# V projected straight into its row form for two head pairs at a time, in a float32 differential-attention and expert kernel

## The reference, cut to what matters

```python
Q = jnp.einsum('bse,hec->bhsc', X, Wq) + bq[None, :, None, :]
K = jnp.einsum('bse,hec->bhsc', X, Wk) + bk[None, :, None, :]
V = jnp.einsum('bse,hed->bhsd', X, Wv) + bv[None, :, None, :]
Q1, Q2 = (Q[..., :d], Q[..., d:])          # d = 64
K1, K2 = (K[..., :d], K[..., d:])
A1 = jnp.einsum('bhqd,bhkd->bhqk', Q1, K1) * s
A2 = jnp.einsum('bhqd,bhkd->bhqk', Q2, K2) * s
P = jax.nn.softmax(A1, axis=-1) - lam * jax.nn.softmax(A2, axis=-1)
O = jnp.einsum('bhqk,bhkd->bhqd', P, V)
```

## Time and profile before

| | us |
|---|---|
| median of 3 runs (2049.75 to 2055.78) | 2054.06 |
| the profiled execution, its own time | 2053.49 |
| span of its trace | 2051.5 |
| PE busy | 1903.1 |
| VectorE busy | 1609.2 |
| ScalarE busy | 1493.6 |
| GpSimd busy | 909.5 |

### The profile page before, as it was taken

One profiled execution on the slowest core, in us unless ns is written; L12 is line 12 of the kernel. 1 busy time (PEld: TensorE's weight loads), 2 busy tenths in 40 slices (PEclk: granted clock), 3 DMA queues, 4 the chain that ended last, 5 costly groups with the idle time before them and its releaser, 6 DMA issues. The chain is left out here.

```text
span 2051.5 us, 39312 instructions
## 1 busy us (share of the span) xinstructions
PE 1903.1 (93%) x10625; PEld 1465.2 (71%) x10625; DVE 1609.2 (78%) x2960; ACT 1493.6 (73%) x3383; POOL 909.5 (44%) x893
## 2 busy tenths in 40 slices
PE   4369999999999999999999999999998699997885
PEld 4347767776777677767767776777675699997885
DVE  5448888888888888888888888888887456664566
ACT  3348888888888888888888888888887466665332
POOL 1234444444444444444444444444433365564676
PEclk9999999999999999999999999999999899999888
DMA  5778888788778777887888787777873866672564
GB/s 174 275 226 215 210 210 215 197 210 213 209 200 212 211 206 204 212 215 198 208 211 215 198 209 212 216 195 209 211 191 78 317 222 235 244 223 98 169 213 125
DMA packets 162207, 421.05 MB, mean 205 GB/s; under 512 B 27794, under 2 KB 69568, under 8 KB 146944
## 3 DMA queue, kind: packets, MB, share of 16 engines
q1 hardware_dynamic: 157408, 410.42, 70.7%
q0 software_dynamic: 4768, 10.25, 1.8%
HBM read 177.53 MB, written 41.72 MB: 107 GB/s over the span
## 5 line engine op out<-in xcount | busy, mean ns | idle before, releaser
L567 POOL TENSOR_TENSOR e<-e,rrec 128x512 f32<-128x512 f32 x512 | 532.1, 1039 | 832.1 <-DVE rrec L683 832.1
L644 ACT ACTIVATE e<-p_score,nmax 128x512 f32<-128x512 f32 x1024 | 695.2, 684 | 136.3 <-DVE nmax L708 135.5
L708 DVE TENSOR_REDUCE nmax<-p_score 128x2 f32<-128x1024 f32 x512 | 626.8, 1224 | 152.8 <-PE p_score L766 148.4
L766 PE MATMUL p_score<-ks,qs 128*128 128x512 f32 x2048 | 575.0, 402 | 6.6 <-ACT e L644 3.8
L754 PE MATMUL p_proj<-xp,w 128*128 (+1 forms) x1920 | 524.6, 409 | 21.2 <-SPq L482 21.2
L766 PEld LDWEIGHTS p_score<-ks,qs 128*128 128x128 f32 x2048 | 369.6, 188 | 180.6 <-ACT e L644 53.9
L754 PEld LDWEIGHTS p_proj<-xp,w 128*128 128x128 f32 x1920 | 339.8, 190 | 80.4 <-SPq L482 21.9
L694 DVE SCALAR_TENSOR_TENSOR pm<-e,coef 128x512 f32<-128x512 f32 x512 | 388.9, 760 | 0.0
L611 ACT COPY pT<-p_tr 128x512 f32<-128x512 f32 x512 | 301.3, 588 | 98.4 <-PE p_tr L776 97.8
L776 PE MATMUL p_tr<-consts,pm 128*128 128x128 f32 x2048 | 307.2, 273 | 2.3 <-ACT pT L611 2.3
L776 PEld LDWEIGHTS p_tr<-consts,pm 128*128 128x128 f32 x2048 | 254.6, 140 | 71.2 <-issue 2.5
(11 more groups left out here) (137 smaller groups left out, 1735.1 us busy)
## 6 DMA issues: line engine op xcount, KB each, us to landing
ks<-k_parts SPq DMA_DIRECT2D x512, 256.0 KB, 4.3
w<-weight_parts_scratch SPq DMA_DIRECT2D x64, 1280.0 KB, 8.1
qs<-q_parts SPq DMA_DIRECT2D x512, 128.0 KB, 2.9
w<-in_w SPq DMA_DIRECT2D x46, 1024.0 KB, 7.7
oT_scratch<-oT SPq DMA_DIRECT2D x64, 256.0 KB, 4.7
oTs<-oT_scratch SPq DMA_DIRECT2D x16, 1024.0 KB, 16.5
ys_scratch<-y SPq DMA_DIRECT2D x23, 256.0 KB
weight_parts_scratch<-n_wt_parts SPq DMA_DIRECT2D x4, 1280.0 KB, 7.3
```

The source lines that it names most:

```text
L567: nc.gpsimd.tensor_tensor(e1, e1, rrec[:, t % 4, 0:1].to_broadcast([P, S]), ALU.mult).then_inc(s_e1, 1)
L644: nc.scalar.activation(ex[:, t % 4, m, :], p_score[t % 2][:, m, :], ACT.Exp, bias=nmax[:, t % 2, m:m + 1], accum_out=rsum[:, t % 4, m:m + ...
L708: nc.vector.tensor_reduce(nmax[:, t % 2, :], p_score[t % 2][:, :, :], AXX, ALU.max, negate=True).then_inc(s_max, 1)
L766: last_op = nc.tensor.matmul(p_score[st % 2][:, m, :], qs[j][u][:, m, qt * P:(qt + 1) * P], ks[j][u][:, m, part, :], start=(part == 0), st ...
```

## The change

V is no longer made transposed. For two pairs at a time (256 columns of V's weights side by side, new tile `wv`), a token tile of 128 columns of `x` is the stationary operand and the weights are the moving one, so that V comes out with tokens on the partitions, as `times_v` wants it. One step (`V_STEP`, 6) of each pair makes two of the four token tiles of the next two pairs: `values`, 12 matmuls of 256 columns. The bias of V lies along the free axis now: a table `bv` of 512 KB is loaded once, and DVE adds it while it copies (`add_bv`, in place of `copy_v`). ACT's copy to `vT` and the transposes "vt" are gone, GpSimd's bias copies too. `PV_STEP` has two runs of two key tiles. The low part of `x` is written over `x` itself (`xl`), the high part has two buffers (`xh`). The attention's loops are written out for all 64 pairs on every engine. The weights of q and k are loaded without those of V; V's come in two transfers for two pairs, in runs of 128 elements on the SBUF side.

```diff
-        ORDER = ("q0", "k0", "q1", "k1", "v", "vt")
-        AT_STEP = {0: "q0", 1: "k0", 2: "q1", 3: "k1", 4: "v", 6: "vt"}
-
-        PV_STEP = {5: (0,), 6: (1,), 7: (2, 3)}
+        ORDER = ("q0", "k0", "q1", "k1")
+        AT_STEP = {0: "q0", 1: "k0", 2: "q1", 3: "k1"}
+        V_STEP = 6
+        PV_STEP = {5: (0, 1), 7: (2, 3)}
...
+def load_v_weights(sp, dst, wp_d, pair, c):
+
+    return sp.dma_start(dst[:, :, :, c, :].bitcast(F32),
+                        wp_d[pair, :, :, WQK:WPAIR].rearrange("p a (k d) -> p a k d", d=P))
... route stage, SyncE
-                sp.dma_start(w_first[j][:, :, :].bitcast(F32), wp_d[j]).then_inc(s_wfirst, 16)
+                sp.dma_start(w_first[j][:, :, :].bitcast(F32), wp_d[j, :, :, 0:WQK]).then_inc(s_wfirst, 16)
+            for it in range(2):
+                for c in range(2):
+                    load_v_weights(sp, wv_first[it], wp_d, 2 * it + c, c).then_inc(s_wfirst, 16)
... attention, SyncE
+            sp.dma_start(bv[:, :], ins["bv"]).then_inc(s_const, 16)
+            def load_wv(it):
+                a = it % 2
+                sp.wait_ge(s_vp, 2 * (it - 2) + 2)
+                for c in range(2):
+                    load_v_weights(sp, wv[a], wp_d, (2 * it + c) % PAIRS, c).then_inc(s_wv[a], 16)
... attention, GpSimd
-                    if t % TPP == 5 and not last:
-                        pair = 2 * it + t // TPP
-
-                        pool.wait_ge(s_lo, 4 * pair + 4)
-                        pool.wait_ge(s_vT, pair + 1)
-                        pair_bias(pair + 2, t // TPP)
... attention, ScalarE
-            def v_bias(pair, j):
-
-                act.wait_ge(s_proj, 6 * pair + 5)
-                b = bias_now[j][:, bias_of["v"]:bias_of["v"] + 1]
-                nc.scalar.activation(vT[:, :], p_proj[0][:, :], ACT.Identity, bias=b).then_inc(s_vT, 1)
... attention, VectorE
-            dve.wait_ge(s_const, 32)
+            dve.wait_ge(s_const, 48)
-            def copy_v(pair, j, fresh):
-                dve.wait_ge(s_proj, 6 * pair + 6)
-                if not fresh:
-                    dve.wait_ge(s_pv, pair - 1)
-                nc.vector.tensor_copy(v[j][:, :, :], p_proj[1][:, :].rearrange("p (k d) -> p k d", d=P)
-                                      ).then_inc(s_v, 1)
+            def add_bv(n):
+
+                it, half = n // 2, n % 2
+                dve.wait_ge(s_vp, n + 1)
+                if it >= 2:
+                    dve.wait_ge(s_pv, 2 * (it - 1))
+                rows = bv[:, 2 * P * (it % QT):2 * P * (it % QT + 1)].unsqueeze(1).to_broadcast([P, 2, 2 * P])
+                nc.vector.tensor_tensor(v[it % 2][:, 2 * half:2 * half + 2, :],
+                                        p_proj[1][:, :].rearrange("p (t d) -> p t d", d=2 * P), rows, ALU.add
+                                        ).then_inc(s_v, 1)
... attention, TensorE
+            def values(n, projected):
+
+                it, half = n // 2, n % 2
+                batch = batch_of(2 * it)
+                pe.wait_ge(s_lo, projected)
+                if n >= 1:
+                    pe.wait_ge(s_v, n)
...
+                for s in range(2):
+                    c = (2 * half + s) * P
+                    for k in range(KT):
+                        for i, (a, b) in enumerate(((0, 0), (0, 1), (1, 0))):
+                            last_op = nc.tensor.matmul(p_proj[1][:, s * 2 * P:(s + 1) * 2 * P],
+                                                       x_part(batch, a, k, c, c + P), wv[it % 2][:, b, k, :, :],
+                                                       start=(k == 0 and i == 0), stop=(k == KT - 1 and i == 2))
+                last_op.then_inc(s_vp, 1)
+            values(0, 4)
+            values(1, 4)
+            for g in range(STEPS):
+                pair, st = g // TPP, g % TPP
+                scores(g)
+                if g >= LAG:
+                    transposes(g - LAG)
+                if st in PV_STEP and pair >= 1:
+                    times_v(pair - 1, PV_STEP[st])
+                if st in AT_STEP and pair + 1 < NPAIRS:
+                    project(pair + 1, AT_STEP[st])
+                if st == V_STEP and pair <= NPAIRS - 3:
+                    values(2 + pair, 4 * (pair + 1) + 4)
```

More of the change, by code:

```diff
@@ L416, in sem @@
             return ctx.enter_context(nc.semaphore(name))
-        bias = sb("bias", [P, PAIRS, 5])
-        bias_of = {"q": 0, "k": 2, "v": 4}
-        bias_now = [sb(f"bias_now{j}", [P, 5]) for j in range(2)]
+        bias = sb("bias", [P, PAIRS, 4])
+        bias_of = {"q": 0, "k": 2}
+        bv = sb("bv", [P, PAIRS * P])
         lam = sb("lam", [P, 1])
@@ L479, in _, with load_w, spread @@
             sp.dma_start(lam[:, :], ins["lam"]).then_inc(s_const, 16)
[L480 to L488, removed]
+            sp.dma_start(bv[:, :], ins["bv"]).then_inc(s_const, 16)
+            def load_w(pair):
+                j = pair % 2
+                sp.wait_ge(s_proj, 4 * (pair - 2) + 4)
+                sp.dma_start(w[j][:, :, :].bitcast(F32), wp_d[pair % PAIRS, :, :, 0:WQK]).then_inc(s_w[j], 16)
+            def load_wv(it):
[3 more added lines that the diff above has]
+                    load_v_weights(sp, wv[a], wp_d, (2 * it + c) % PAIRS, c).then_inc(s_wv[a], 16)
+            def spread(u, what, pair):
+                j = pair % 2
                 n = 4 * pair + 2 * u + (what == "k")
@@ L504, in spread, with store_o @@
                                          a[:, :, :].bitcast(F32)).then_inc(s_dup[j][u], 16)
+            def store_o(pair):
+                j = pair % 2
+                sp.wait_ge(s_o, pair + 1)
+                dst = oT_d[pair % PAIRS, :, batch_of(pair) * S:(batch_of(pair) + 1) * S]
+                sp.dma_start(dst, oT[j][:, :]).then_inc(s_ost[j], 16)
             for u in range(2):
                 for what in "qk":
[L508 to L531, removed]
+                    spread(u, what, 0)
+            for pair in range(NPAIRS):
+                if pair + 2 < NPAIRS:
+                    load_w(pair + 2)
+                if pair % 2 == 0 and pair // 2 + 2 < ITERS:
+                    load_wv(pair // 2 + 2)
+                if pair + 1 < NPAIRS:
+                    for u in range(2):
+                        for what in "qk":
+                            spread(u, what, pair + 1)
+                if pair >= 2:
+                    store_o(pair - 2)
@@ L532, in _ @@
+            store_o(NPAIRS - 2)
+            store_o(NPAIRS - 1)
             for j in range(2):
-                sp.wait_ge(s_ost[j], 16 * (ITERS + 1))
+                sp.wait_ge(s_ost[j], 16 * ITERS)
         @block.gpsimd
         def _(pool):
[L537 to L541, removed]
@@ L647, in _ @@
-            looped(act, ITERS, body, peel_last=True)
-            g = ITERS * 2 * TPP
-            for t in range(LAG):
-                lst = TPP - LAG + t
-                copy_pT(g - LAG + t, 1, lst // QT, lst % QT, 2 * ITERS - 1, False)
-            copy_o(2 * ITERS - 2, 0)
-            copy_o(2 * ITERS - 1, 1)
+                if pair >= 2:
+                    act.wait_ge(s_ost[pair % 2], 16 * (pair // 2))
+                nc.scalar.copy(oT[pair % 2][:, :], p_pv[:, :]).then_inc(s_o, 1)
+            for what in ORDER:
+                high_part(0, what)
@@ new lines, in _ @@
+            for g in range(STEPS):
+                pair, st = g // TPP, g % TPP
+                if st == 0 and pair >= 2:
+                    copy_o(pair - 2)
+                what = AT_STEP.get(st - 1)
+                if what and pair + 1 < NPAIRS:
+                    high_part(pair + 1, what)
+                if g >= LAG:
+                    copy_pT(g - LAG)
+                for m in range(2):
+                    act.wait_ge(s_max, g + 1)
+                    if m == 0 and g >= 4:
+                        act.wait_ge(s_comb, g - 3)
+                    nc.scalar.activation(ex[:, g % 4, m, :], p_score[g % 2][:, m, :], ACT.Exp,
+                                         bias=nmax[:, g % 2, m:m + 1],
+                                         accum_out=rsum[:, g % 4, m:m + 1]).then_inc(s_exp, 1)
@@ L674, in copy_v @@
-            def copy_v(pair, j, fresh):
-                dve.wait_ge(s_proj, 6 * pair + 6)
-                if not fresh:
-                    dve.wait_ge(s_pv, pair - 1)
-                nc.vector.tensor_copy(v[j][:, :, :], p_proj[1][:, :].rearrange("p (k d) -> p k d", d=P)
-                                      ).then_inc(s_v, 1)
-            def reciprocals(g, b):
+                b = bias[:, pair % PAIRS, bias_of[what[0]] + u:bias_of[what[0]] + u + 1]
+                nc.vector.scalar_tensor_tensor(out=parts[what[0]][u][:, 1, :], in0=p_proj[n % 2][:, :], scalar=b,
+                                               in1=parts[what[0]][u][:, 0, :].bitcast(F32),
+                                               op0=ALU.add, op1=ALU.subtract).then_inc(s_lo, 1)
@@ L690, in combine @@
+            def combine(g):
                 dve.wait_ge(s_e1, g + 1)
```

(30 more changed lines are left out.)

308 lines of the change are left out of this document (129 added, 179 removed).

## The result

The changed kernel takes 2018.97 us (median of 4 runs, 2017.94 to 2021.58) against 2054.31 before; the ratio is 0.9834, with a 95% interval from 0.9815 to 0.9852. The forecast was 2019. In a later session of 5 runs beside other kernels it took 2018.75 (ratio 0.9828, interval 0.9815 to 0.9842). The profiled execution has a span of 2016.4 us, 35.1 less than before.

What follows compares the result with a forecast made beforehand. PE's own pace was taken to bound the kernel. 36.6 us from 61 pairs plus 2.5 at the ends minus 4 at the start gave 35 off the profiled 2053.49: 2018.4, as a median 2019; range 2006 to 2038.

Steps and rivals of the forecast that it cites:

- Steps 4 to 7: PE's second half of a pair: from 11.60 us to 1.27 + 3.41 + 2.89 + 3.33 = 10.90, 0.70 less.
- The term for `values`: Step 6 on PE: twelve new 256-column matmuls take 1.42 to 1.52 us, taken as 1.50.
- The experts' 118 ns: Time per matmul of the same type and shape in the experts' stage (48 in 5.66 us), used to price `values`.
- "v" itself: V's old matmuls, dropped from step 4: no saving, since the new ones cost 1.50 us against 1.48.
- the joined key tiles: Two key tiles together in step 5 instead of one each in steps 5 and 6: 1.87 us against 1.01 twice.
- The walk to step 5's wait: Other engines followed through PE's shorter step 4: waits of 0.2 us in every second pair, 0.1 a pair on the mean.
- two waits of 0.1: Step 5: first its scores wait for step 3's exponentials, then its transposes for ACT's copy of step 4's transposes.
- Steps 0 to 3: PE's first half of a pair: keeps its work and its 11.08 us.
- The 61 pairs: Pairs 2 to 62 in attention, each a net 0.60 us shorter: 36.6 us.
- the first pair and the last two: Attention's ends: no product with V in the first pair, no V made in the last but one; 2.5 us saved.
- The start: Before the first scores: a cost of 4 us (1 to 7), 3 for more V weights in route, 1 in attention.
- DVE's addition: `add_bv` in step 0 takes 0.74 us against the copy's 0.68, at no cost since DVE has slack there.

Runs made afterwards that it cites:

- e1: Kernel before the change with attention's loops written out for all 64 pairs, nothing else changed; 2054.65 us against 2054.61.
- e2: Kernel before the change with key tiles 0 and 1 joined in step 5, none in step 6, V still transposed; 2033.79 us.
- e3: Changed kernel with the key tiles of steps 5 and 6 apart again, so V's new form alone; 2040.14 us.
- e7: Changed kernel without GpSimd's split of x in attention, every batch projected from the first batch's parts; 2015.67 us.
- e9: Changed kernel with the two runs of key tiles in steps 4 and 7 instead of 5 and 7; 2015.21 us.
- e4: Changed kernel with all four key tiles of the product with V in step 4; 2034.08 us.
- e6: Changed kernel with V's first weights loaded between the route stage's later parts and a semaphore of its own for `bv`; 2016.53 us.
- e10: Changed kernel run again, unaltered, beside another kernel on the same chip; 2018.75 us.
- e5: Changed kernel with all four key tiles of the product with V in step 7; 2074.76 us.

## Why the prediction was right, point by point

**What bounds the kernel.** PE's own pace, confirmed from both sides: e1 changes code and branches and nothing moves, e2 takes out of a pair what its expectation priced at 0.32 us of PE's work, and the pair becomes 0.30 shorter.

**Steps 4 to 7.** Forecast 10.90 without waits; measured in odd pairs 1.28 + 3.44 + 2.90 + 3.32, together 10.95. The 0.03 of step 5 lie between its transposes and its products (0.56, not 0.53). The term for `values` (1.50) measured 1.51, the mean of 48. The experts' 118 ns carried over to the new place; the 109 ns that come out of the Trainium skill's figure for a matmul taken alone (TensorE: Matmul & The Clock Gate, Back-to-back issue gap) do not hold here: from one low-part matmul of `values` to the next, three matmuls on, it is 0.358 us on the mean of 144, 119 ns each.

**Where the saving sits.** The prediction said that "v" itself saves nothing and that it is "vt" and the joined key tiles. e2 and e3 bear that out, and weigh the two as its sum did not: of 35 us, 21 come from one line of a table that V's new form does not need, and 14 from V's form.

**The walk to step 5's wait.** Forecast 0.2 in every second pair, in two waits of 0.1; measured 0.11, in the second alone. The first needed DVE late by 1.41; it was 1.26, and 0.11 of that difference is the combine, 0.90 rather than 1.01. Why it was shorter is open. e7 shows the split as the cause, e9 that the wait has a place where it is not paid.

**A term that was missing.** Steps 0 to 3 were to keep 11.08 and take 11.14 (11.09 before by the same means). It is not the loops, since e1 has 11.09, and not the joined tiles, since e2 has 11.10. It is found with the projection from the two tiles `xh` and `xl`: steps 1 to 3 take 8.27 or 8.28 in all kernels that have it, also in e4, whose step 0 is shorter for other reasons, and 8.23 and 8.24 in those that have not. Some 0.02 of it lie in the projection of step 1 (1.464 before, 1.480 now). No run changes that alone, so its cause is open; it costs 62 x 0.05 = 3 us. Together the pair saved 0.54 where 0.60 was forecast: 36.2 us from the first to the last scores (131.40 to 1573.33 before, 134.23 to 1539.94 after), against 39.1. The 61 pairs gave 33.6 (forecast 36.6), the first pair and the last two 2.6 (2.5).

**The start.** Forecast 4, measured 2.83, from two terms that were both mis-sized: 3 for bytes in the route stage, 1 in attention. The first was 0.3, since PE's first projection starts at 117.69 against 117.40, and the second 2.5. What counts is the wait for `bv`, since ACT's first high part stands at 122.35 against 120.37, and V's matmuls in a chain with DVE. What the four loads take is SyncE's time, 6.88 us to issue, 4.42 of them for one load, and the next weight load of the route stage comes 2 us later. e6 takes both away and gives back 3.2 us of the first scores.

**The sum.** 2.83 - 36.22 = -33.4 by the trace up to the last scores, -35.1 over the whole span: 1.7 us lie behind the last scores. They are no gain of the change: from the last scores to the end it is 478.2 before, 476.5 in this trace and 478.0 in e10's, of the same kernel. The error of 0.0 is luck in that these differences (2.9 less saved, 1.2 less lost, 1.7 found) cancel.

**DVE's addition.** 0.68 us like the copy, not the 0.74 allowed.

## What to carry to other kernels

When one engine is full, count the time between the starts of its groups, and look at the borders between kinds of work: here two runs of products instead of three were worth more (21 us) than a projection that needs no transposes (14 us, with its dearer start counted). Before work is moved between steps of a software pipeline, walk the other engines through the two steps around each short one: the same work on PE gave 2034 or 2075 us depending on where one long step stood (e4 and e5), and both lost to the changed kernel, by 15 and 56 us, with less work on PE. A long step where the second engine has most to do (step 4 in e9) took a wait of 0.11 us away from every second pair; that is one case, and e4 shows that the step after it can be made too short.

## What was not expected of the hardware

Instructions delivered in sequence (70 packets of together 1.15 MB on this queue in e1, 15 of together 0.25 before) cost nothing while the DMA engines are at 0.79 of their share. One of four loads with runs of 128 elements took 4.42 us to issue in SyncE's list, the others 0.7 to 1.0, at a DMA share of 0.86 (84 to 117.7 us by the busy times); in the whole kernel the median of the same load is 0.69. Full queues alone don't explain it: in e6 the same four take 3.63 together at a share of 1.04 (97 to 110 us), and none of its 64 takes more than 1.58. The cause is open.
